# Output pieces loaded ahead of a query's stores, and a matrix's low parts made by VectorE instead of GpSimd

## The reference

```python
x = x + attn_a(layernorm(x), Wqkv, Wo)       # 32 heads of 16, one key/value head, ALiBi, causal
x = x + ffn(layernorm(x), c1_w, c2_w, w1, w2t)
x = x + attn_b(layernorm(x), wq, wk, wv, wo) # 32 query and 8 key/value heads of 128, RoPE, window of 128
x = x + ffn(layernorm(x), c1_w, c2_w, w1, w2t)

def ffn(x):                                  # x: 2048 x 512
    inter = x @ c1_w.T @ c2_w.T              # 2048 x 1792
    idx = argmax of inter in each block of 32 columns     # 56 rows per token
    h = relu(w1[idx] . x)                    # a token's 56 hidden values
    return h @ w2t[idx]                      # the sum of the 56 rows
```

## Time and profile before

| | before |
|---|---|
| median of 3 runs | 2777.52 us (2772.59 to 2779.67) |
| profiled execution | 2770.34 us, span 2768.6 us |
| mean granted clock of PE, share of full speed | 0.964 |
| busy: PE, DVE, ACT, POOL | 94%, 62%, 47%, 38% |

### The profile page before, as it was taken

One profiled execution on the slowest core, in us unless ns is written; L12 is line 12 of the kernel. 1 busy time (PEld: TensorE's weight loads), 2 busy tenths in 40 slices (PEclk: granted clock), 3 DMA queues, 4 the chain that ended last, 5 costly groups with the idle time before them and its releaser, 6 DMA issues. The chain is left out here.

```text
span 2768.6 us, 41665 instructions
## 1 busy us (share of the span) xinstructions
PE 2594.3 (94%) x14444; PEld 2026.0 (73%) x14444; DVE 1721.9 (62%) x3488; ACT 1309.1 (47%) x2952; POOL 1054.8 (38%) x938
## 2 busy tenths in 40 slices
PE   4798988889999889999999998999999999799999
PEld 2444443467778678888888876888888888577777
DVE  3674656167777566666566656666666666577775
ACT  2354546332222356566666655566665666232221
POOL 2111122175333344444444423445444443473322
PEclk7899999899999999999999999999999999899999
DMA  5334242220000210111000110111001100300000
GB/s 164 107 94 122 64 117 62 74 84 1 1 0 1 63 31 9 38 38 38 30 18 27 38 39 1 39 39 38 30 8 38 38 23 1 119 1 16 16 15 16
DMA packets 113464, 117.42 MB, mean 42 GB/s; under 512 B 6245, under 2 KB 85989, under 8 KB 113317
## 3 DMA queue, kind: packets, MB, share of 16 engines
q1 hardware_dynamic: 112448, 115.51, 13.7%
q10 hardware_dynamic: 900, 0.40, 0.1%
HBM read 92.09 MB, written 22.68 MB: 41 GB/s over the span
## 5 line engine op out<-in xcount | busy, mean ns | idle before, releaser
L2018 POOL TENSOR_TENSOR rope_straight<-rope_straight,rope_crossed 128x512 f32<-128x512 f32 x160 | 207.0, 1294 | 528.7 <-DVE rope_crossed L1802 528.7
L592 POOL TENSOR_TENSOR f_hidden_low<-f_hidden,f_hidden_high 128x256 fp32r<-128x256 f32 x224 | 183.0, 838 | 400.8 <-ACT f_hidden_high L532 400.6
L1820 DVE TENSOR_TENSOR o_low<-o_sum,o_high 128x512 fp32r<-128x512 f32 x128 | 88.5, 692 | 316.6 <-ACT o_high L1998 316.3
L1029 DVE TENSOR_REDUCE a_max<-a_work 128x1 f32<-128x384 f32 (+3 forms) x352 | 205.3, 635 | 111.8 <-PE a_work L917 110.1
L1912 ACT ACTIVATE probs<-probs,exp_bias 128x256 f32<-128x256 f32 (+1 forms) x512 | 240.3, 471 | 3.3 <-DVE exp_bias L1785 3.2
L1154 ACT ACTIVATE a_probs<-a_scores 128x512 f32<-128x512 f32 x320 | 173.8, 596 | 134.5 <-PE a_scores L931 67.5
L1923 ACT CAST q_high<-rope_straight 128x512 fp32r<-128x512 f32 x128 | 79.5, 621 | 298.6 <-POOL rope_straight L2018 298.6
L1917 ACT ACTIVATE probs<-probs,exp_sum_inverse 128x256 f32<-128x256 f32 (+1 forms) x512 | 205.2, 472 | 32.4 <-DVE exp_sum_inverse L1790 32.4
L532 ACT CAST f_hidden_high<-f_hidden 128x512 fp32r<-128x512 f32 x112 | 69.5, 620 | 309.1 <-PE f_acc L296 170.8
L1622 PE MATMUL w_sum<-o_high,wo_high 128*128 128x512 f32 x512 | 204.9, 400 | 8.7 <-DVE xt L1827 4.8
L1622 PE MATMUL w_sum<-o_high,wo_low 128*128 128x512 f32 x512 | 204.0, 398 | 0.0
(11 more groups left out here) (240 smaller groups left out, 7529.3 us busy)
## 6 DMA issues: line engine op xcount, KB each, us to landing
a_queries<-a_q_stacked SPq DMA_DIRECT2D x16, 1024.0 KB, 6.3
wq_raw<-in_L_attn_b_wq SPq DMA_DIRECT2D x32, 512.0 KB, 3.7
wo_raw<-in_L_attn_b_wo SPq DMA_DIRECT2D x16, 1024.0 KB, 6.4
a_q_stacked<-a_q_part_high SPq DMA_DIRECT2D x32, 256.0 KB
f_w_raw<-in_L_ffn_w SPq DMA_DIRECT2D x14, 512.0 KB, 10.3
f_w_raw<-in_L_ffn_w2t SPq DMA_DIRECT2D x14, 512.0 KB, 11.1
a_q_stacked<-a_q_part_low SPq DMA_DIRECT2D x16, 256.0 KB
wkv_raw<-in_L_attn_b_wk SPq DMA_DIRECT2D x16, 256.0 KB, 6.4
```

What stands on the lines that cost most here:

```text
L592: e.tensor_tensor(hl[:, j % 2, cols], hm[:, cols], f32(hh[:, j % 2, cols]), ALU.subtract).then_inc(hl_ready, 1)
L1029: e.tensor_reduce(mx[:, t % 2, to:to + nh], bank, AX.X, ALU.max).then_inc(work_free[k], 1)
L2018: e.tensor_tensor(ra[:, slot], ra[:, slot], rb[:, slot], ALU.add).then_inc(roped, 1)
```

## The change

In `causal_attention`, for b = 1 and 2, SP issues the four `load_out(b-1, m)` directly behind `store_inverses(b-1)`, ahead of `send_queries(b+1, 2)`; they stood behind it. In both `ffn` blocks, in the first batch, the low parts of w2 of chunks 1 to 6 are made by DVE with one instruction of 1024 columns for each chunk, in chunk c behind keep(2c) and find_max(c+1, 0); POOL made them with four instructions of 256 columns in chunk c-1. POOL's own `low_w2(0)`, ahead of the batches, stays.

```diff
@@ ffn, block.vector @@
+            def low_w2(i):
+                e.wait_ge(w2_high, i + 1)
+                e.tensor_tensor(w2l[:, 2 * i:2 * i + 2], w2_raw[:, 2 * i:2 * i + 2], f32(w2h[:, 2 * i:2 * i + 2]), ALU.subtract)\
+                    .then_inc(w2_low, 4)
...
                         if c + 1 < NCH:
                             find_max(it, c + 1, half, chain)
+                        if first and c and half == 0:
+                            low_w2(c)
@@ ffn, block.gpsimd @@
                     if first and c + 1 < NCH:
                         if c + 2 < NCH:
                             low_w1(c + 2)
-                        low_w2(c + 1)
@@ causal_attention, block.sync @@
                 if b:
                     send_max(b, 2)
                     store_inverses(b - 1)
+                    for m in range(DT):
+                        load_out(b - 1, m)
                 if more:
                     send_queries(b + 1, 2)
                 if b == 0:
                     send_max(0, 2)
-                for m in range(DT) if b else ():
-                    load_out(b - 1, m)
                 if more:
                     send_queries(b + 1, 3)
                     queries_stored(b + 1)
```

## The result

| | before | after |
|---|---|---|
| median | 2778.6 us (2772.6 to 2781.4, 4 runs) | 2748.3 us (2740.2 to 2754.6, 4 runs) |
| ratio | | 0.9898, 95% interval 0.9872 to 0.9924 |
| profiled execution | 2770.34 us, span 2768.6 | 2754.62 us, span 2752.8 |
| mean granted clock | 0.964 | 0.965 |

The changed kernel is 1.0% faster, 30 us between the medians, 28 by the ratio; forecast were 24.4. Two more comparisons of the same kernel gave 0.9895 (0.9879 to 0.9910) and 0.9898 (0.9881 to 0.9916). The profiled execution is the slowest of its four, and that of before, 2770.34 us, is faster than all four runs of before; so the spans lie only 16 us apart and not 28. 5 us of that difference arise ahead of b = 1, where nothing was changed.

What follows compares the result with a forecast made beforehand. PE, busy 94% of the span, was taken as the bound, so only its waits and low-clock stretches could be won. Attention 14.2 + feed-forward 10.2 = 24.4 us off the 2777.52 us median gave 2753.1, range 2740 to 2768.

Steps and rivals of the forecast that it cites:

- Attention, the first two waits: b = 1: PE's waits for exponentials and ahead of Wo 0 go, Wo 0 at full clock: 2.68 + 2.45 + 1.5 = 6.6 us.
- the slow stretch: PE's matmuls at a lower clock after a wait, as in Wo 0 and the feed-forward; 1.5 us taken for each.
- SP is late next: Attention: SP's queue at send_max(1, 3) limits the gain; SP earlier by 7.7 us, PE by 7.0, counted as 7.1.
- The rival with 2767 us: SP gives the gain back at send_max, attention gains nothing: 2777.5 - 10.2 = 2767 us; chance 0.12.
- a wait of 3 us or more: Attention: a wait of PE for send_max this long was named as a sign that the prediction is wrong.
- The sum for attention, 14.2: Moving the loads gains 7.1 us in b = 1 and again in b = 2; bounds nothing and 17 us.
- for b = 2 PE's pattern recurs: Attention, b = 2: PE waits as in b = 1, with 2.85 us in the last wait, so 7.1 us again.
- Feed-forward, (b): Ahead of sum_squares in chunk 2: mask waits of 2.54 and 2.72 us go, with a slow stretch of 1.5 us each.
- Feed-forward, (a): Ahead of sum_x in chunk 0: POOL ends 2.8 us earlier, the mean's waits go; 2.3 us in f1_, 2.7 in f2_.
- Chunks 4 to 6: DVE's price: 0.3 us at chunk 4's bank and 1.0 us up to stack_t, charged in each feed-forward block.
- The net for the feed-forward, 10.2: Moving w2's low parts to DVE gains 4.8 us in f1_ and 5.4 in f2_; bounds 2 and 14 us.
- The rival built on holding: POOL holds DVE's subtractions, some 4.3 us each, none hidden: slower, 2802 us; decides from about 3.0 us each; chance 0.03.

Runs made afterwards that it cites:

- e6: Changed kernel with send_max(b, 3) issued between the stores of qt = 0 and qt = 1; median 1.9 us faster, not measurably different from the changed kernel.
- e7: Changed kernel with DVE's six subtractions of each block put where its timeline shows it idle; not measurably different from the changed kernel.
- e1: Kernel before with only the four load_out issued ahead of send_queries(b+1, 2); 2756.07 us against 2773.96, ratio 0.9928.
- e4: Changed kernel with each of DVE's 12 subtractions done twice; 2760.90 us, ratio 0.9938 to the kernel before.
- e9: Kernel before with the four load_out issued behind queries_stored and the two load_queries that follow; 2797.78 us, ratio 1.0082, 22.9 us slower.
- e2: Kernel before with only w2's low parts of the first batch moved to DVE; 2765.17 us against 2773.96, ratio 0.9966.
- e3: Kernel before with low_w2 still on POOL, but behind sum_x in chunk 0 and the three sum_squares in chunk 2; 2770.51 us, ratio 0.9983.
- e12: The changed kernel as it is, measured again beside other experiments; the changed kernel's two further comparisons gave 0.9895 and 0.9898.
- e5: The changed kernel as it is, measured again beside e6 to e8; the changed kernel's two further comparisons gave 0.9895 and 0.9898.
- e8: Changed kernel with the edits of e6 and e7 together; not measurably different from the changed kernel, where 8 us were expected.
- e11: Changed kernel with e6's send_max move and e7's subtraction places, pairs 1 and 2 left as changed; median 2.6 us faster, not measurably different.
- e10: Changed kernel without DVE's 12 subtractions, high parts used for low ones; 2736.37 us beside the changed kernel's 2747.42, ratio 0.9859 to before.

## Why the prediction was right, point by point

**Attention, the first two waits.** As forecast: both gone, Wo 0 at full clock, `out_tile` at 238.03. The forecast was 237.3, but in this trace SP's queue ran 5.2 us later at the inverses' store. The pieces came after 5.0 us and not after the 9.0 that I had carried over. The size was too small: by the end of Wo 0, PE had gained 7.7 us and not 6.6. I had counted the slow stretch in Wo 0 but not the one behind the wait for the exponentials (clock 0.55 before, 1.00 after). There PE gained 1.5 us more, less the 0.35 us of that wait which stayed.

**SP is late next.** Right in kind: the row that waits for `send_max(b, 3)` is still there in both batches, and e6, which moves nothing else, removes it. The size is right by two errors. The waits one by one, in ns, of before and after (shortest, median, longest; by their places these are b = 0, 1 and 2):

```profile
L1311 SPq EVENT_SEMAPHORE  x3: 4912/9933/10391, 133.6 to 365.2; - x3
L1317 SPq EVENT_SEMAPHORE  x3: 4917/5165/5920, 137.8 to 362.4; - x3
```

b = 0's wait is 4.9 us. I had 4.5, because I took 10.4 for b = 1 too. The wait became 4.8 us shorter in b = 1 and 4.5 in b = 2, not 5.9. But the last store was also issued some 3 us earlier in b = 1, where I had 1.8, so SP gained 8.0 us where 7.7 were forecast. PE kept 7.4 us there, as much as `send_max(1, 3)` moved. How near SP is shows in the wait for that row in equal code: in b = 1 it is 0.16 us in e7, 0.20 in e1, 0.74 in after and 3.06 in e4. The rival with 2767 us fell by e1, but the sign that I had named for it, a wait of 3 us or more, came in this one execution.

No run here tests the rule of the Trainium skill that I weighed ("DMA: Bandwidth & Descriptors", Queues, rings and completion order: a DMA engine takes the descriptors of one queue in ring order). In e9 the stores waited 5.9 us at the longest, but the 2 MB were issued only after they had landed. In the changed kernel the 2 MB had landed when POOL began its last `out_tile`, at 244.6, and the last query's stores went only after that.

**The sum for attention, 14.2.** In the means of the table b = 1 gives 97.0 - 89.2 = 7.7 us and b = 2 108.9 - 101.9 = 7.1, 14.8 together. Without e4 it would be 8.4 and 7.5, together 15.9. But e1's medians say 17.9 and its ratio 20.0, and its interval begins at 16.1. So 14.2 was too low, and the profiled stretches account for 15 or 16 of these 18 to 20 us; the rest stays open. Of the 8.7 us that b = 1 gained in the trace of after, 1.3 came in at its end (302 to 315 us of before), where nothing was changed and a stretch of lower clock was longer in before (0.53 in 313.6 to 315.8 us; the same matmuls have 1.00 in after). That part is luck. The step least sure was "for b = 2 PE's pattern recurs": in before's trace b = 2 was 4 us shorter than in e2 and e3, so from that trace alone the gain there would be 4.3 us.

**Feed-forward, (b).** Right: 2.5 or 2.7 for the mask and 1.5 for the slow stretch were forecast, less 0.2. The mean gain is 11.40 - 7.17 = 4.2 us in f1_ and 24.49 - 20.06 = 4.4 in f2_.

**Feed-forward, (a).** Too large: 2.3 and 2.7 us forecast, 28.80 - 27.28 = 1.5 and 25.66 - 24.63 = 1.0 found. The failed step is the chain behind `low_hidden(2)`. I let DVE go on at 585.4 as soon as POOL was done, but did not count that this `low_hidden(2)` gets longer beside the subtraction, 2.86 us. DVE's next `keep_hidden` waits 0.73 us for it, and PE 1.34 and 1.57 us for z, where I expected 0.5. In f2_ a slow stretch can follow that wait. (a) takes 25.1 us in the four traces (after, e2, e6, e12) whose wait for z is 1.57 us, and there the granted clock of the 3.6 us behind it is 0.53 to 0.55. It takes 22.8 in e5 with a wait of 1.23, and 22.6 and 22.9 in e8 and e11 with 1.07 and 1.35; in these three that clock is 1.00.

**Chunks 4 to 6.** Too dear: 0.3 and 1.0 us charged in each block, 0.45 found in each ("rest"). The wait for `stack_t` is 1.14 and 1.17 us, not 1.9. DVE gained back more of its time than I reckoned, since it meets POOL's work less often; `normalise`'s L376, for one, takes 2.29 us instead of 2.71.

**The net for the feed-forward, 10.2.** 5.3 + 5.0 = 10.3 us by the table, 8.8 by e2's medians (5.5 to 13). It is right because two errors cancel. Against e10, where the work is on neither engine, the gross gain is 16.4 us and DVE's price 6.1; the terms of my sum are 13.2 and 3.0. The durations were nearly as forecast (1.22 us where I took 1.2, and 1.76 beside POOL where I took 1.6). The waits were not: 1.34 and 1.57 us for z instead of 0.5, 1.14 and 1.17 for `stack_t` instead of 1.9. What I took too favourably was how much of DVE's work lies in its idle time.

"SBUF — State Buffer" (Who interferes with whom) of the Trainium skill says that a VectorE instruction with two SBUF inputs and a GpSimd one that reads SBUF exclude each other for a whole instruction. The rows agree: POOL's pair got 1.21 us longer, which is one subtraction of DVE, and DVE's instruction 0.54. The rival built on holding (3.0 us and more for each subtraction) did not come.

**The total.** 24.4 us forecast, 28 measured by the ratio; by the medians of the two parts alone, 17.9 in attention (14.2 forecast) and 8.8 in the feed-forward (10.2 forecast). Attention gave more than forecast and the feed-forward less, and the two errors partly cancel in the total.

## What to carry to other kernels

In this kernel, a queue written out in one order cost twice, as a large load stood between two stores that something waits for: the load's user waited, and the stores' user too (e1), and with the load behind both, PE waited 18 to 19 us (e9). Work that left POOL helped by more (e2, 9 us) than a new order on it (e3, 3.5 to 4.7), as what follows it there is waited for; and its price on the new engine is to be read from the whole chain, with both engines' instructions lengthened where they meet. A wait count taken from one execution is uncertain by what the clock did in it; a second trace of equal code shows by how much.

## What the runs showed that I had not expected

Stretches of lower clock move from one execution to the next. With equal code, b = 2 took 106.1 us in before and 110.6 and 110.1 in e2 and e3, and (a) of f2_ 22.8 to 25.1 in the three traces of the changed kernel. A term of 1.5 us for such a stretch is a mean and not a reading.

Small waits of PE were replaced rather than removed: in e7 and e11 the 1.17 us for `stack_t` went, and 0.95 to 1.15 us came in elsewhere. With PE busy for 91.5, DVE for 82.3 and POOL for 58.8 of 98.5 us, the first batch has several chains within 1 us of each other.
